# The conditioning MLP with its weights as stationary blocks, and a new order of transfers and of VectorE's early work

## What is computed

```python
h = noise_encoding(t, 128)            # sin and cos of 5000 * t * freqs
h = silu(h @ W1 + b1)                 # 128 -> 512
h = h @ W2 + b2                       # 512 -> 512
scale = (h @ Wsc + bsc)[:, None, :]   # 512 -> 256
shift = (h @ Wsh + bsh)[:, None, :]
out = silu(scale * layer_norm(x, gamma, beta) + shift)    # mean, variance over positions and features
out = out @ W_in + b_in               # 256 -> 256
out = silu(scale * layer_norm(out, gamma, beta) + shift)
out = out @ W_out + b_out
return out + x
```

## Time and profile before

| what | us |
| --- | --- |
| median of 3 runs | 103.71 (102.8 to 103.94) |
| span of the profiled execution | 101.5 |
| median less that span | 2.2 |
| TensorE matmul busy | 88.8 |
| VectorE busy | 80.9 |
| ScalarE busy | 58.1 |
| GpSimd busy | 39.7 |

### The profile page before, as it was taken

One profiled execution on the slowest core, in us unless ns is written; L12 is line 12 of the kernel. 1 busy time (PEld: TensorE's weight loads), 2 busy tenths in 40 slices (PEclk: granted clock), 3 DMA queues, 4 the chain that ended last, 5 costly groups with the idle time before them and its releaser, 6 DMA issues.

```text
span 101.5 us, 1109 instructions
## 1 busy us (share of the span) xinstructions
PE 88.8 (88%) x267; PEld 41.3 (41%) x268; DVE 80.9 (80%) x197; ACT 58.1 (57%) x174; POOL 39.7 (39%) x40
## 2 busy tenths in 40 slices
PE   5995999989999999976579995995998699999990
PEld 2351173365355544224243352451643245444450
DVE  1510617999979989999999899999799967789951
ACT  5030024244774898397679149939952999966600
POOL 1000027359244069039972992950493020120000
PEclk9999999985589999999985999999999999999999
DMA  0799999993000000000005000500500050230484
GB/s 4 146 354 399 374 384 397 397 408 150 0 3 0 0 3 0 0 0 0 0 0 207 0 0 0 207 0 0 185 28 3 0 207 0 85 125 0 159 300 161
DMA packets 6598, 11.89 MB, mean 117 GB/s; under 512 B 960, under 2 KB 2752, under 8 KB 6592
## 3 DMA queue, kind: packets, MB, share of 16 engines
q1 hardware_dynamic: 6592, 11.82, 32.4%
HBM read 7.63 MB, written 4.19 MB: 116 GB/s over the span
## 4 chain that ended last, share of the span: by engine, by line
DVE 41%; PE 31%; POOL 8%; DMA 7%; issue 5%; ACT 4%; SPq 2%; DVEq 0%; ACTq 0%
PE big L581 21%; DVE act L413 8%; DVE act L421 7%; DMA x_sb<-x_dram 7%; DVE bn L338 5%; DVE act L383 5%; DVE act L374 4%; DVE act L366 3%; POOL act L222 3%; POOL act L225 3%; DVE o_sb L429 3%; DVE wrow L389 2%; ACT squares L275 2%; PE big L550 2%; ACT act L257 2%
## 5 line engine op out<-in xcount | busy, mean ns | idle before, releaser
L257 ACT ACTIVATE act<-act,cond 128x256 f32<-128x256 f32 x64 | 35.7, 590 | 19.8 <-DVE act L421 11.3
L581 PE MATMUL big<-act,win_sb 128*128 128x512 f32 x64 | 33.2, 644 | 0.9 <-DVE act L413 0.8
L581 PE MATMUL big<-act,wout_sb 128*128 128x512 f32 (+1 forms) x68 | 31.0, 605 | 2.0 <-DVE act L413 1.8
L581 PEld LDWEIGHTS big<-act,wout_sb 128*128 128x128 f32 x68 | 12.9, 198 | 15.1 <-issue 11.4
L581 PEld LDWEIGHTS big<-act,win_sb 128*128 128x128 f32 x64 | 11.9, 204 | 12.9 <-issue 9.7
L222 POOL TENSOR_TENSOR act<-act,gamma_sb 128x512 f32<-128x512 f32 x10 | 13.7, 1382 | 7.7 <-DVE act L366 7.7
L275 ACT ACTIVATE squares<-big,shift 128x256 bf16<-128x256 f32 x32 | 15.0, 470 | 1.9 <-PE big L581 0.7
L225 POOL TENSOR_TENSOR act<-act,beta_sb 128x512 f32<-128x512 f32 x10 | 15.0, 1510 | 0.5
L421 DVE SCALAR_TENSOR_TENSOR act<-act,rstd,beta_sb 128x512 f32<-128x512 f32 x16 | 14.5, 949 | 0.1
L229 POOL TENSOR_TENSOR rstd<-var,minus_half 128x2 f32<-128x2 f32 x8 | 5.9, 733 | 22.1 <-DVE var L402 22.1
L338 DVE BATCH_NORM_STATS2 bn<-x_sb 128x6 f32<-128x512 f32 x16 | 10.2, 680 | 4.6 <-DMA x_sb<-x_dram 4.6
(11 more groups left out here) (56 smaller groups left out, 64.5 us busy)
## 6 DMA issues: line engine op xcount, KB each, us to landing
x_sb<-x_dram SPq DMA_DIRECT2D x8, 512.0 KB, 10.7
out_dram<-o_sb SPq DMA_DIRECT2D x15, 256.0 KB, 2.1
w_sb<-w_dram SPq DMA_DIRECT2D x1, 1024.0 KB, 6.0
wss_sb<-wsc_dram SPq DMA_DIRECT2D x1, 512.0 KB, 7.8
wss_sb<-wsh_dram SPq DMA_DIRECT2D x1, 512.0 KB, 8.8
w_sb<-w_dram SPq DMA_DIRECT2D x1, 256.0 KB, 2.7
gamma_sb<-gamma_dram SPq DMA_DIRECT2D x1, 256.0 KB, 8.9
beta_sb<-beta_dram SPq DMA_DIRECT2D x1, 256.0 KB, 8.5
```

The costliest lines, as they stand in the source:

```text
L257: return nc.scalar.activation(buf[:, c, b], buf[:, c, b], ACT.Silu, bias=cond[:, 1, c, i:i + 1], scale=cond[:, 0, c, i:i + 1], **kw)
L581: mm = nc.tensor.matmul(acc[:, c, b * S:(b + n) * S], w[:, k, c * P:(c + 1) * P], act_in[:, k, b:b + n].rearrange("p b s -> p (b s)"), sta ...
```

## The change

1. The hidden product and that of scale and shift are made by `features_product`: 4x4 blocks of 128x128 of the weights stationary, 16 samples moving. The result has the features on partitions at once. copy_rows, transposed, their tiles, semaphores and the identity in `enc` go.
2. t, enc and the biases are issued from ScalarE's queue; on SP's the order becomes w1, x0, w2, gamma, x1, beta, wsc, wsh, w_in, x2 ...
3. VectorE adds no phase to the angle: it clamps to bounds that differ by partition, and the sine's bias adds it (one operation less).
4. VectorE's and TensorE's early order changes; the chain of group 2 goes behind Y0; w_in's row sums move to VectorE as one tensor_reduce behind cond; other numbers of warm matmuls.

```diff
-CHAIN_OF_STEP = {1: 3, 3: 4, 5: 5}
+CHAIN_OF_STEP = {0: 2, 1: 3, 3: 4, 5: 5}
-WARM_AFTER = 4
-WARM_BETWEEN = 2
+WARM_BEFORE_HIDDEN = 4
+WARM_BEFORE_COND = 6
...
-            sp.dma_start(t_sb[:], t.rearrange("(a b) -> a b", a=1).to_broadcast([P, B])).then_inc(t_in, 16)
-            sp.dma_start(enc_sb[:], enc).then_inc(enc_in, 16)
-            sp.dma_start(bias_sb[:], biases).then_inc(bias_in, 16)
             sp.dma_start(w1_sb[:], w1).then_inc(w1_in, 16)
+            load_x(0)
             sp.dma_start(w2_sb[:], w2.rearrange("(k p) n -> p k n", p=P)).then_inc(w2_in, 16)
-            load_x(0)
+            sp.dma_start(gamma_sb[:], gamma).then_inc(gamma_in, 16)
+            load_x(1)
+            sp.dma_start(beta_sb[:], beta).then_inc(beta_in, 16)
...
-            act.wait_ge(enc_step, 8)
-            nc.scalar.activation(h0[:], angle[:], ACT.Sin).then_inc(h0_ready, 1)
+            act.wait_ge(enc_step, 7)
+            nc.scalar.activation(h0[:], angle[:], ACT.Sin, bias=enc_sb[:, COL_PHASE:COL_PHASE + 1]).then_inc(h0_ready, 1)
...
-            copy_rows(h2_rows, big[1], h2_rows_mm, h2_rows_ready)
-
-            act.wait_ge(win_in, 16)
-            for k in range(C):
-                if k > 0:
-                    act.wait_ge(wsum_ready, k)
-                nc.scalar.activation(squares[:], win_sb[:, k], ACT.Identity, accum_out=wsum[:, k:k + 1]).then_inc(wsum_ready, 1)
-            act.wait_ge(wsum_ready, C)
-            copy_rows(cond_rows, big[2], cond_rows_mm, cond_rows_ready)
             act.wait_ge(cond_ready, 1)
...
+            dve.wait_ge(win_in, 16)
+            nc.vector.tensor_reduce(wsum[:], win_sb[:], AX.X, ALU.add).then_inc(wsum_ready, 1)
...
+            def features_product(acc, w, h):
+
+                for n in range(KH):
+                    for k in range(KH):
+                        mm = nc.tensor.matmul(acc[:, 0, n * B:(n + 1) * B], w(k, n), h[:, k], start=(k == 0), stop=(k == KH - 1))
                 return mm
...
-            warm(4)
+            warm(WARM_BEFORE_HIDDEN)
+            pe.wait_ge(consts_set, 1)
+            mean1(0)
             pe.wait_ge(h1_ready, KH)
             pe.wait_ge(w2_in, 16)
...
+            features_product(big[1], lambda k, n: w2_sb[:, k, n * P:(n + 1) * P], h1).then_inc(h2_mm, 1)
             variance1(0)
...
+            mean1(1)
+            warm(WARM_BEFORE_COND)
+            variance1(1)
             pe.wait_ge(h2_ready, 1)
...
+            features_product(big[2], lambda k, n: wss_sb[:, k, n // C, (n % C) * P:(n % C + 1) * P], h2).then_inc(cond_mm, 1)
```

More of the change, by code:

```diff
@@ L244, in _ @@
         def _(act):
+            act.dma_start(t_sb[:], t.rearrange("(a b) -> a b", a=1).to_broadcast([P, B])).then_inc(t_in, 16)
+            act.dma_start(enc_sb[:], enc).then_inc(enc_in, 16)
+            act.dma_start(bias_sb[:], biases).then_inc(bias_in, 16)
             nc.scalar.preload_act_table_set("silu_and_others")
-            act.wait_ge(enc_step, 8)
-            nc.scalar.activation(h0[:], angle[:], ACT.Sin).then_inc(h0_ready, 1)
+            act.wait_ge(enc_step, 7)
+            nc.scalar.activation(h0[:], angle[:], ACT.Sin, bias=enc_sb[:, COL_PHASE:COL_PHASE + 1]).then_inc(h0_ready, 1)
+            act.wait_ge(bias_in, 16)
             act.wait_ge(h1_mm, 1)
-            act.wait_ge(bias_in, 16)
             for k in range(KH):
@@ L435, in _ @@
             stats1_deviation(0)
+            weigh_gamma(0)
             stats1_variance(0)
@@ L444, in _ @@
             stats1(1)
+            weigh_beta(0)
             stats1_deviation(1)
-            weigh_gamma(0)
-            weigh_beta(0)
+            weigh_gamma(1)
             stats1_variance(1)
-            stats1(2)
+            centre1(1)
+            weigh_beta(1)
             dve.wait_ge(cond_mm, 1)
@@ L454, in _ @@
                                     ALU.add).then_inc(cond_ready, 1)
-            centre1(1)
-            stats1_deviation(2)
-            weigh_gamma(1)
+            dve.wait_ge(win_in, 16)
+            nc.vector.tensor_reduce(wsum[:], win_sb[:], AX.X, ALU.add).then_inc(wsum_ready, 1)
             dve.wait_ge(mean_b_mm, 1)
             nc.vector.tensor_scalar(mean_b[:], stat2[:, 0:1], 1.0 / C, None, ALU.mult).then_inc(mean_b_ready, 1)
-            dve.wait_ge(wsum_ready, C)
+            dve.wait_ge(wsum_ready, 1)
             nc.vector.tensor_scalar(wmean[:], wsum[:], float(P) / (S * D), None, ALU.mult).then_inc(wmean_ready, 1)
@@ L465, in _ @@
                                     ALU.subtract).then_inc(b_in_c_ready, 1)
-            weigh_beta(1)
-            stats1_variance(2)
+            stats1(2)
             dve.wait_ge(wmean_ready, 1)
@@ L470, in _ @@
             mean2_partial(0)
+            stats1_deviation(2)
+            mean_shift2(0)
             stats1(3)
-            mean_shift2(0)
+            stats1_variance(2)
             centre1(2)
-            stats1(4)
-            mean2_partial(1)
             weigh_gamma(2)
             weigh_beta(2)
+            mean2_partial(1)
+            stats1(4)
             stats1_deviation(3)
@@ L645, in _ @@
             pe.wait_ge(wsh_in, 16)
-            for k in range(KH):
-                mm = nc.tensor.matmul(big[2][0:B, 1], h2[:, k], wss_sb[:, k].rearrange("p a n -> p (a n)"),
-                                      start=(k == 0), stop=(k == KH - 1))
-                if k == KH - 1:
-                    mm.then_inc(cond_rows_mm, 1)
-                if k == 1:
-                    mean1(1)
-            variance1(1)
-            transposed(big[2], cond_rows, cond_rows_ready).then_inc(cond_mm, 1)
-            mean1(2)
-            warm(WARM_AFTER)
-            variance1(2)
+            features_product(big[2], lambda k, n: wss_sb[:, k, n // C, (n % C) * P:(n % C + 1) * P], h2).then_inc(cond_mm, 1)
             pe.wait_ge(win_in, 16)
@@ L696 @@
     enc = np.zeros((P, N_ENC), np.float32)
-    enc[:B, COL_EYE:] = np.eye(B, dtype=np.float32)
     enc[:, COL_FREQ] = np.tile(freqs, 2)
@@ L700 @@
     enc[half:, COL_PHASE] = math.pi / 2
+    enc[:, COL_LOW] = -PI_BELOW - enc[:, COL_PHASE]
+    enc[:, COL_HIGH] = PI_BELOW - enc[:, COL_PHASE]
     arrays = {
```

37 lines of the change are left out of this document (4 added, 33 removed).

## The result

The changed kernel takes 123.66 us (median of 4 runs, 122.07 to 124.06), the kernel before in the same session 103.41 (4 runs, 102.8 to 103.94): a ratio of 1.190, 95% interval [1.175, 1.205]. The forecast had the direction right and the time 12.5 us too low, outside its range. The profiled execution of after is the highest of its runs (124.06, span 122.3); that of before has a span of 101.5. In every run here that has both, the time stands 1.7 to 1.9 us above the span, not the 2.2 that the prediction added. Spans differ by 20.8 us and medians by 20.3. Some executions run a few per cent slower than the fastest of the same kernel, with a lower mean clock: the ratios leave these out on both sides (e1 has only one other and no ratio), so they stand a little off the quotient of the medians, and the profiled executions of after, e1 and e9 are among them.

A forecast was written before the change was run, and what follows sets the result against it. No engine was full overall, but VectorE, busy 19.59 of 20.40 us from 28.8, could not win back lateness. +5.1 to cond, +1.5 VectorE's order, +0.9 TensorE's: 103.71 + 7.5 = 111.2 us, range 104 to 113.3.

The forecast's parts named there:

- 1.3 us of cover: Before the hidden product: h1 waits 1.3 us for w2, which also hides any later landing of the small transfers.
- w2 at 8.6: Transfers: w2 lands at 8.6 us, from 9.95 less 1.37, so the hidden product starts no earlier.
- TensorE's clock: Early TensorE work: short matmuls, then 2.8 us of nothing, drop the clock to half between 11 and 16 us.
- the clock already low in product one, up to 32 x 0.09 = +2.9: Bound on the hidden product: its 32 records at half clock add up to 2.9 us, one half likely.
- Loads at half clock: Stationary-weight products: a load takes 0.20 us at half clock, making a product 6.4 us against 3.6 at full clock.
- Rival 3: Second product: weight loads don't slow with the clock, so it takes 3.4 to 3.6 us; 108.3 us, chance 0.03.
- Rivals 1 and 2: Second product at full clock: clock holds (105.2 us, chance 0.18), or warm matmuls raise it in time (106.5 us, 0.07).
- rival 4: Behind cond: clock holds and the way follows ScalarE and TensorE, not VectorE; faster, 102.1 us, chance 0.12.
- mean1(1): TensorE waits here 2.8 us for VectorE's statistics, with warm matmuls, variance1(1) and the second product queued behind.
- From cond to normalise2(0): Stretch behind cond: VectorE's order adds 1.5 us and TensorE's 0.9; normalise2(0) comes at 43.7 against 36.2.
- a second fall while TensorE waits in mean1(3), +1.7: Bound behind cond: the clock falls again while TensorE waits for statistics in mean1(3), adding 1.7 us.
- VectorE has nothing to spare to catch up: Behind normalise2(0): the code is the same and VectorE cannot win back the 7.5 us of lateness.

The follow-up runs named there:

- e1: The changed kernel with t, enc and the biases back at the head of SP's queue; median 119.26 us.
- e9: The kernel before with only the changed kernel's order of the large transfers; 105.43 us, ratio 1.016.
- e5: e1 with the products made the old way (weights moving, row copies, transposes), new order kept; 117.94 us, ratio 1.120.
- e3: The kernel before with only both products made with stationary blocks; 107.39 us, ratio 1.042.
- e2: The kernel before with only t, enc and the biases moved to ScalarE's queue; 108.35 us, ratio 1.055.
- e8: e1 with mean1(1), six warm matmuls and variance1(1) behind the second product, and pair 1's variance, centring and beta behind cond; 117.14 us, ratio 1.139.
- e6: e1 with stats1(4) moved ahead of gamma, beta and the second mean2_partial; 117.68 us, ratio 1.143.
- e10: e5 with group 2's chain back ahead of Y0 and stats1(2), (3), (4) at their old places; 110.31 us, ratio 1.071.
- e4: e1 with 25 more warm matmuls: two ahead of each quarter of both products, nine ahead of mean1(1); 122.40 us, ratio 1.183.

## Why the prediction failed

Along before, e9, e5, e1, after, each kernel carries one part more, and the starts of cond add up. The shares are of single profiled executions and of this order of adding; the last column has the differences of the lowest runs (102.44, 104.37, 115.18, 116.73, 122.07) beside them:

| part | at cond | from cond to normalise2(0) | lowest runs |
| --- | --- | --- | --- |
| new order of the large transfers, w2 behind x0 (e9 less before) | +3.66 | -0.71 | +1.9 |
| new order of TensorE and VectorE, mean1(1)'s wait and all the rest (e5 less e9) | +2.19 | +6.76 | +10.8 |
| stationary blocks (e1 less e5) | +4.26 | -0.58 | +1.6 |
| small transfers on ScalarE's queue (after less e1) | +2.79 | +2.28 | +5.3 |
| sum | +12.90 | +7.75 | +19.6 |

Both ways of counting have the new order as the largest part and the small transfers at about 5 us. The blocks' share isn't settled: 3.7 us at normalise2(0) in the profiles, 1.6 by the lowest runs, 4.0 where they stand alone (e3).

**The transfers: wrong, the first failure.** The step "That also covers the three small transfers should they land later among w1 and x0's packets" gave them 1.3 us of cover. They landed 1.8, 3.3 and 4.9 us later after issue than before, the angle started 3.35 later, and TensorE went idle for 3.45. The cover, the wait for w2, was real as long as h1 came by 8.6; h1's product began at 8.96. Issued from SP ahead of w1, the three had no large transfer ahead of them; from ScalarE's queue they were in flight beside w1 and x0, and took 4.3 to 6.9 us against 2.0 to 2.5. The section "Issuing engines are not separate DMA queues" of the Trainium skill's "DMA: Bandwidth & Descriptors" says that transfers of several engines interleave on the same DMA engines; the longer landing times agree. That the large transfers beside them make them late, and not ScalarE's queue itself, is argued: no run has them on that queue alone. e2 prices the step at 4 to 5 us.

**w2 at 8.6: wrong size.** It took 7.7 us from issue in after (issued 1.65, so landed near 9.4) and the product was later than that anyway. The sum of bytes alone did not give the time. In e9 and e1, where the small ones are on SP, the product that waits for it starts at 10.81 and 10.98.

**TensorE's clock: falls as said, but before product one.** "the clock already low in product one, up to 32 x 0.09 = +2.9" was a bound, and it was what happened, at +3.4: hidden product 12.6 to 19.6 against 8.6 to 12.2 forecast. That is 4.0 us of start and 3.4 of length, which is the whole miss at cond but 0.4 (the forecast's 26.7 is cond's end, which came at 34.53). e3 shows that without any late transfer the clock falls inside product one.

**Loads at half clock: right.** 0.20 taken, 0.22 measured (6.95/32), 6.4 and 7.0 a product. Rival 3 is ruled out by all of e1, e3 and after. The rule named with it, of the Trainium skill's "TensorE: Matmul & The Clock Gate", section "LDWEIGHTS" (columns/1.2 ns, 0.107 us for 128), fits the loads at full clock only. Rivals 1 and 2 fell with the clock, rival 4 with cond.

**mean1(1): right.** 2.8 us forecast, 2.33 measured. By e8's profile it costs 5.2 at cond with its warm matmuls and its place, of which 2.0 reach normalise2(0).

**From cond to normalise2(0): mechanism right, size wrong.** Forecast 17.0, measured 22.3, both from cond's end. By the forecast's own steps, counted from there: group 2's rstd was to be done at +8.8 and was at +9.8, as Y0's halves took 3.75 and 2.79, partly or wholly at half clock (+1.0). Gamma, beta and mean2_partial(1) ended at +11.2 in the forecast and at +14.1: beta took 1.57 and not 0.75 and wrow 1.22 and not 0.16, beside GpSimd (+1.8). That makes TensorE's wait in mean1(3) 4.96, the clock fell again ("a second fall while TensorE waits in mean1(3), +1.7"), and from stats1_deviation(3) to normalise2(0) it took 6.1 and not 3.9 (+2.2). With 0.25 between these this is the 5.3. e6 shows that the wait is VectorE's order (1.30 when stats1(4) goes ahead); e10 undoes the order for group 2, and normalise2(0) comes 5.3 earlier.

**"VectorE has nothing to spare to catch up": right.** Behind normalise2(0) every profiled execution takes 65.2 to 65.4 us.

So the first step that failed is the cover of 1.3 us, a term put at nothing for the small transfers: their lateness (3.35 us at the angle) went through to product one and, with the clock's early fall, set its start 4.0 us late. The clock in product one, the second fall and the stalls beside GpSimd were named as bounds, and each went beyond its own (3.4 for 2.9, 2.2 for 1.7, 1.8 for 1). All upward bounds together make 117.1 us, and the range stopped at 113.3. Even that sum leaves 6.6 us of the 12.5, so the miss was not bad luck within the terms named.

## What to carry to other kernels

A cover of a microsecond for a small transfer that starts the longest chain is no cover, when the change also takes it from the head of the queue: price it with the large transfers in flight. Where short matmuls and waits alternate on TensorE, work the stretch out with the clock low first, and take that as the forecast if any wait ahead of it grows. Add up the upward bounds of a chain before choosing the range: here three came at once, each larger than its bound. Moving a product that a whole group of work waits for behind a long one costs on every engine in turn: undoing it (e10) brought 5 us, the form of the products 4.0 where it stood alone (e3). And look at several executions before reading a share of a few us off two profiles: e5's own runs lie up to 5.9 us apart.

## What the runs showed of the hardware

- The clock fell in e3 at 11.8 behind 3.20 us in which TensorE was busy 3.15, mostly with 16-column f32 matmuls, and in before at 21.9 behind 3.40 us with 3.01 busy. In after it fell at 7.8, with TensorE idle, and in e4 at 9.4, in a wait for a transfer.
- The same instructions with the same transfers saw it fall at different times: e5 at 19.2 us and e10 at 11.0, e1 at 12.2 and e6 at 9.2.
- A 128x128 f32 load record with its 16-column matmul takes 0.12 us at 2.4 GHz (eight in 0.96, e1) and 0.22 at 1.2 GHz (32 in 6.95, after): the load slows with the clock.
- VectorE's operations with two SBUF tiles as inputs took longer beside GpSimd's: in e5 a four-element wrow took 1.22 us and not 0.16 and ended at 40.11, GpSimd's L226 at 40.09; beta took 1.57 and not 0.75, begun at 37.40 within GpSimd's L223 (36.72 to 38.42). The Trainium skill, "SBUF — State Buffer", "SBUF: two separate sides", describes an exclusive lock on a port pair that the two share; the trace agrees in both places.
